# Moving five sine evaluations of the weight preparation ahead of chunk 0's first exponential

## The reference

```python
def step(carry, inp):                  # 16 chunks of 256 rows, 8 heads
    mem, z = carry
    q_s, k_s, v_s = inp                # xn @ Wq, xn @ Wk, xn @ Wv
    sq = elu(q_s) + 1.0
    att_mem = sq @ mem / (sq @ z)
    sk = elu(k_s) + 1.0
    mem = mem + einsum('bhlk,bhlv->bhkv', sk, v_s)
    z = z + sk.sum(axis=-2)
    att = softmax(q_s @ k_s.T * scale) @ v_s
    return (mem, z), gate * att_mem + (1.0 - gate) * att

real = einsum('bti,io->bto', xn, cos(theta + theta_noise))   # the FFN
imag = einsum('bti,io->bto', xn, sin(phi + phi_noise))
ffn  = sqrt(real * real + imag * imag)
out  = x + attention(xn) @ Wo + ffn                          # xn = layernorm(x)
```

## Time and profile before

| | |
|---|---|
| time, median of 2 runs | 1429.98 us (1428.96 to 1431.01) |
| time of the profiled execution | 1431.08 us |
| its span, slowest core (4) | 1429.5 us |
| spans of the eight cores | 1418.5 to 1429.5 us |
| mean granted clock of TensorE, by core | 0.776 to 0.786 |
| busy: PE, DVE, ACT, POOL | 746.4, 751.7, 346.8, 226.6 us |

### The profile page before, as it was taken

The page is one execution under the profiler, slowest core; times in us unless marked ns, Lnnn a source line. Parts: engine busy times, 40 slices in busy tenths (PEclk is TensorE's granted clock), DMA queues, the critical chain, the costliest instruction groups (busy, mean ns, idle before and its releaser), DMA issues.

```text
span 1429.5 us, 14772 instructions; the slowest of 8 cores (1418.5 to 1429.5 us)
## 1 busy us (share of the span) xinstructions
PE 746.4 (52%) x5125; PEld 406.6 (28%) x5125; DVE 751.7 (53%) x1409; ACT 346.8 (24%) x837; POOL 226.6 (16%) x127
## 2 busy tenths in 40 slices
PE   0301574746656464646637365665646464654753
PEld 0200232423233232323224142323224242422321
DVE  2013464655656565664566565565656566456540
ACT  1034132230403122040312213040312214040222
POOL 1011011030211102030111103020111203011113
PEclk9855586877869697886969688887969788796967
DMA  9656300101010010101010010101001010100001
GB/s 167 158 122 146 85 3 1 61 0 60 3 59 3 1 61 0 62 1 60 2 37 25 0 61 1 60 2 59 3 4 58 1 62 0 59 3 30 2 1 59
DMA packets 18123, 56.51 MB, mean 40 GB/s; under 512 B 1217, under 2 KB 5249, under 8 KB 18050
## 3 DMA queue, kind: packets, MB, share of 16 engines
q0 software_dynamic: 8000, 20.97, 7.2%
q1 hardware_dynamic: 10050, 34.59, 6.9%
HBM read 41.98 MB, written 16.78 MB: 41 GB/s over the span
## 4 chain that ended last, share of the span: by engine, by line
PE 38%; DVE 29%; ACT 12%; DMA 7%; issue 7%; DVEq 5%; POOL 1%; ACTq 1%; POOLq 1%
PE pb L123 10%; PE pb L492 8%; ACT e_bf L323 8%; PE pb L376 6%; DVE pT_sb L642 5%; DVE negm L613 4%; PE pb L387 4%; PE pb L399 3%; DVE m2t L658 3%; DVEq L657 3%; DMA stage<-th 3%; DVE attT_bf L680 3%; DVE xnT_sb L565 3%; PE pb L434 2%; DVE out_sb L158 2%
## 5 line engine op out<-in xcount | busy, mean ns | idle before, releaser
L253 POOL TENSOR_TENSOR stage<-fscr 128x1024 f32<-128x1024 bf16 x32 | 63.2, 1974 | 1026.8 <-ACT fscr L138 791.9
L123 PE MATMUL pb<-sin_r,xnT_sb 128*128 128x512 bf16 x512 | 142.2, 441 | 99.0 <-ACT fscr L138 99.0
L323 ACT ACTIVATE e_bf<-pb,negms 128x256 bf16<-128x256 f32 x256 | 117.4, 485 | 157.1 <-DVE negms L618 157.0
L492 PE MATMUL pb<-wo_r,attT_bf 128*128 128x512 bf16 x256 | 113.1, 621 | 71.4 <-DVE attT_bf L680 71.4
L123 PE MATMUL pb<-cos_r,xnT_sb 128*128 128x512 bf16 x512 | 145.9, 449 | 0.0
L642 DVE CAST pT_sb<-pb 128x512 bf16<-128x512 f32 x128 | 79.4, 683 | 112.8 <-PE pb L434 112.8
L376 PE MATMUL pb<-xnT_sb,wq_b 128*128 128x256 bf16 x512 | 87.5, 353 | 80.8 <-DVE xnT_sb L565 59.0
L307 ACT ACTIVATE scr<-scr 128x1024 f32<-128x1024 f32 x16 | 16.9, 1057 | 424.5 <-DVE scr L573 424.4
L138 ACT ACTIVATE fscr<-pb 128x512 bf16<-128x512 f32 x128 | 73.1, 596 | 145.3 <-PE pb L123 132.8
L123 PEld LDWEIGHTS pb<-sin_r,xnT_sb 128*128 128x128 bf16 x512 | 54.5, 110 | 186.5 <-issue 148.4
L422 PE MATMUL pb<-kT_bf,qT_bf 64*128 64x256 bf16 x256 | 21.4, 283 | 162.3 <-DVE sk_bf L595 118.6
(11 more groups left out here) (95 smaller groups left out, 1132.5 us busy)
## 6 DMA issues: line engine op xcount, KB each, us to landing
x_sb<-x SPq DMA_DIRECT2D x16, 1024.0 KB, 5.0
y<-out_sb SPq DMA_DIRECT2D x16, 1024.0 KB, 5.2
stage<-th POOLq DMA_DIRECT2D x2, 1024.0 KB, 22.5
stageB<-th POOLq DMA_DIRECT2D x2, 1024.0 KB, 23.0
stage<-thn POOLq DMA_DIRECT2D x2, 1024.0 KB, 10.8
stageB<-thn POOLq DMA_DIRECT2D x2, 1024.0 KB, 11.7
stage<-ph POOLq DMA_DIRECT2D x2, 1024.0 KB, 6.9
stageB<-ph POOLq DMA_DIRECT2D x2, 1024.0 KB, 7.1
```

Source lines behind the costliest of these rows:

```text
L123: li = t_.matmul(pb[6 + half][:, :], xnT_sb[:, ppf + 256 * dt + 128 * u: ppf + 256 * dt + 128 * u + 128], w_s[:, 1024 * dt + 512 * half: 1 ...
L253: g.tensor_mul(stage[:, 0:1024], fscr[:, 0:1024], fscr[:, 0:1024])
L323: sc.activation(e1_bf[:, 2048 * u + 256 * h: 2048 * u + 256 * h + 256], sl, AF.Exp, bias=negms[:, c:c + 1], scale=0.125, accum_out=den[:, ...
L492: li = t_.matmul((bh0 if half == 0 else bh1)[:, :], attT_bf[:, 128 * ft:128 * ft + 128], wo_r[:, 1024 * ft + 512 * half: 1024 * ft + 512 * ...
```

## The change

The Sins 3 to 7 leave their places in chunk 0 and follow Sins 0 to 2, so that all eight stand in a row ahead of the chunk loop. The five calls inside the loop go. Nothing else differs; the lists of PE, DVE, POOL and SP are the same.

```diff
@@ -299,20 +299,16 @@
                 sc.drain().then_inc(s_lnc, 1)
 
             ln_chain(0)
-            for n in range(3):
+            for n in range(2 * NTH):
                 emit_sin(n)
             for t in range(nch):
                 pp = 2048 * (t % 2)
                 sc.wait_ge(s_mq, t + 1)
                 sc.activation(scr[:, 1024:2048], scr[:, 0:1024],
                               AF.Exp).then_inc(s_eq, 1)
-                if t == 0:
-                    emit_sin(3)
                 sc.wait_ge(s_mk, t + 1)
                 sc.activation(scr[:, 3072:4096], scr[:, 2048:3072],
                               AF.Exp).then_inc(s_ek, 1)
-                if t == 0:
-                    emit_sin(4)
                 for u in range(2):
                     sc.wait_ge(s_mx, 2 * t + u + 1)
                     for h in range(8):
@@ -325,8 +321,6 @@
                                       sl, AF.Exp, bias=negms[:, c:c + 1],
                                       scale=0.125, accum_out=den[:, c:c + 1])
                     sc.drain().then_inc(s_e1, 1)
-                    if t == 0:
-                        emit_sin(5) if u == 0 else (emit_sin(6), emit_sin(7))
                     if t >= 1:
                         ffn_evac(sc, t - 1, u)
                         if u == 1:
```

## The result

| | before | after |
|---|---|---|
| time, median | 1431.58 us (10 runs) | 1470.57 us (11 runs) |
| ratio, with its 95% interval | | 1.0267 (1.0246 to 1.0288) |
| profiled execution | 1431.08 us | 1469.26 us |
| its span, slowest core | 1429.5 us (core 4) | 1467.7 us (core 7) |
| spans of the eight cores, mean | 1424.1 us | 1464.2 us |

The changed kernel is 2.7% slower, 38 to 39 us. The forecast was 1470 us.

A forecast was written before the change was run, and what follows sets the result against it. No engine is full; a hand-over from engine to engine bounds the kernel. The profiled 1431.08 us plus chunk 1's 40.3 us delay gives 1471.4, or 1470.3 against the median, written 1470; range 1460 to 1479.

The forecast's parts named there:

- (a): On ACT in the head, Sins 3 to 7 need no table loads; Sin 7 starts at 149.73 instead of 153.60.
- (b): Chunk 0 waits for the whole Sin stream; Exp q comes at 152.95, where it was at 89.38.
- (c): Chunk 0 then runs without pauses; chunk 1 begins at 211.73 instead of 171.47, 40.3 us later.
- (d): From chunk 1 to the end nothing recovers the delay; the 40.3 us are carried to the end.
- The range's allowances for TensorE's clock: In the range's low end: 6.4 us less for chunk 1's clock and about 2.5 for part of chunk 0's.
- A: Rival in the head: table loads decide, eight fewer take off 10.3 us, time 1420.8; 2 in 100.
- B: Rival: the stream runs faster with nothing beside it; within 2% needs it ending 11.7 us earlier; 2 in 100.
- C: Rival: TensorE's clock pays back in chunks 0 and 1, 14.6 us at most, time 1455.7; 5 in 100.
- D: Rival: loads stay before the Sins, Sin 7 is 3.9 later, time 1475.9, at most near 1479; 4 in 100.

The follow-up runs named there:

- Experiment 5: Changed kernel with a tiny extra Exp behind each of Sins 2 to 6, putting table loads back; 1479.88 us against 1432.64.
- Experiments 1 to 4: Kernel before with Sin 3, Sins 3-4 or Sins 3-5 ahead of Exp q, or Sins 3-7 behind chunk 0's last Exps; ratios 1.0003, 1.0056, 1.0146, 0.9921.
- experiment 1: Kernel before with only Sin 3 moved ahead of Exp q; 1430.94 us against 1429.55, ratio 1.0003.
- 9: Kernel before with chunk 0's Exps as early as their data, plus SP's load of x for chunk 2 held until Sin 6 is done; 1389.41 us against 1432.45.
- experiments 1 to 3: Kernel before with Sin 3, Sins 3-4 or Sins 3-5 moved ahead of Exp q; ratios 1.0003, 1.0056 and 1.0146.

## Why the prediction was right

**(a) The stream.** Expected periods without loads 14.66, 15.03, 14.27, 14.56; on core 7 they are 15.03, 14.34, 14.51 and 14.13, together 58.01 against 58.52. Sin 7 at 149.45 (149.73 expected). Experiment 5 confirms the direction of the load's price and its size within 0.1 us a load in the stream, and speaks against the 2.66 us of the Trainium skill.

**(b) and (c) Chunk 0.** Exp q 152.68 (152.95), Exp k 157.55 (157.83), score Exps 164.13 and 178.68 (164.39, 178.93), chunk 1 at 211.50 (211.73). Each step is within 0.3 us. Experiments 1 to 4 show the mechanism by moving one Sin, two, three and none: the covered first Sin, the price of the next ones, and the pauses of the kernel before as a gain when they go. They also correct the prediction's opening sentence, that a delay anywhere in the kernel is paid in full: Exp q's 14 us in experiment 1 cost nothing.

The closeness has some luck in it. The prediction was worked out on core 4 of one execution, and the slowest core after is 7. The start of chunk 1 varied between cores from 165.96 to 173.99 before and from 204.16 to 212.54 after, because their streams run at different speeds; on core 7 the shift is 37.5, on core 4 35.2, on the mean of all eight 39.4. The mean span rose by 40.1 us.

**(d) Nothing gives it back.** From chunk 1's start to the end 1256.2 us, expected 1258: right within the spread between cores. The range's allowances for TensorE's clock weren't needed; the granted clock in chunk 0 and chunk 1 was 0.53 and 0.72 against 0.53 and 0.73.

**Rivals.** A, the table loads as what decides: eight went, and nothing was gained on the path beyond (a). (Its 1420.8 is counted from the profiled execution; against the median, as the forecast is, it would be 1419.7. Neither is near.) B, a stream that speeds up by itself: Sin 2 to Sin 6 took 58.0, not under 50. C, the clock: above. D, loads that stay: none stayed. The reason given against B, that work beside the stream hardly touches it, holds for DVE and PE (9), but a load of x beside it cost 2.2 us; in the kernel before none ran there.

## What to carry to other kernels

An order on one engine is a set of waits for all: put work whose input comes late from a slow stream behind the work that others are waiting for, and ask for each item when its consumer first needs it (here the Sins' consumer came only in chunk 1). Fewer table loads on an engine that idles are worth only those loads that stand behind a landed transfer. What a delay costs isn't proportional: in experiments 1 to 3 it was free up to the next pause, and then cost in full.

## What was not expected of the hardware

The transfers of the weight stream do not run at one speed on all cores: in the profiled execution of the changed kernel Sin 7 started between 142.60 and 151.20 us, four cores near 144 and four near 150. Most of that gap was there early: Sin 2 started near 82.4 on the first four and near 87.2 on the others. The slowest core (7) is a late one, but core 0, an early one, ended only 1.3 us ahead of it. Which cores are late changes between the profiled executions of the kernels (1, 3, 4 and 7 before; 1, 2, 5 and 7 after); why wasn't tried.
